# Later factor loads on the second DMA queue, and slot 0's sums in other PSUM banks

## The reference

```python
def _L0_cond_ref(x, w, b):          # depthwise causal conv1d
    y = jax.lax.conv_general_dilated(x, w, window_strides=(1,), padding=[(K - 1, 0)], feature_group_count=D, ...)
    return y + b

def _L0_ffn_ref(x, w_router, w_experts):
    logits = jnp.einsum('bsh,eh->bse', x, w_router)
    idx = jnp.argmax(logits, axis=-1)
    all_out = jnp.einsum('bsh,efh->bsef', x, w_experts)
    return jnp.take_along_axis(all_out, idx[:, :, None, None], axis=2)[:, :, 0, :]

x = x + _L0_ffn_ref(_L0_cond_ref(x, cond_2048[:, None, :], L0_cond_b), L0_ffn_w_router, L0_ffn_w_experts)
```

## Time and profile before

| | |
|---|---|
| median of 3 runs | 513.11 us (511.46, 513.11, 513.98) |
| the profiled execution | 512.61 us |
| its span, first to last instruction | 510.8 us |
| TensorE busy | 502.5 us, 98% |
| VectorE, ScalarE, GpSimd busy | 56%, 29%, 26% |
| convolution, first to last matmul | 4.86 to about 123 us |
| expert slots | 123.51 to about 505 us |
| mean granted TensorE clock | 0.997 |

### The profile page before, as it was taken

One profiled execution on the slowest core, in us unless ns is written; L12 is line 12 of the kernel. 1 busy time (PEld: TensorE's weight loads), 2 busy tenths in 40 slices (PEclk: granted clock), 3 DMA queues, 4 the chain that ended last, 5 costly groups with the idle time before them and its releaser, 6 DMA issues.

```text
span 510.8 us, 9483 instructions
## 1 busy us (share of the span) xinstructions
PE 502.5 (98%) x2764; PEld 435.5 (85%) x2765; DVE 287.6 (56%) x418; ACT 150.5 (29%) x255; POOL 133.2 (26%) x148
## 2 busy tenths in 40 slices
PE   8999999999999999999999999999999999999995
PEld 8999999998888888888888888888888888888884
DVE  4947373769885233599753422863266343472961
ACT  2444444286101001365620000610043010340710
POOL 0004325063622111323311312203122322122222
PEclk9999999999999999999999999999999999999998
DMA  8977999999779999699998664695649655534445
GB/s 290 411 221 212 398 282 405 348 346 309 264 253 283 341 350 299 184 348 358 327 395 249 175 198 123 202 372 177 185 133 354 221 165 158 169 116 130 145 142 165
DMA packets 59623, 130.31 MB, mean 255 GB/s; under 512 B 12752, under 2 KB 32720, under 8 KB 59600
## 3 DMA queue, kind: packets, MB, share of 16 engines
q1 hardware_dynamic: 41696, 70.12, 44.3%
q0 software_dynamic: 14832, 54.27, 29.6%
q10 hardware_dynamic: 3072, 5.65, 3.5%
HBM read 94.56 MB, written 35.45 MB: 255 GB/s over the span
## 4 chain that ended last, share of the span: by engine, by line
PE 93%; DMA 5%; issue 0%; POOL 0%; DVE 0%; DVEq 0%; ACT 0%; SPq 0%; POOLq 0%
PE ps L858 75%; PE ps L814 18%; DMA y_sorted<-rows,pos_i 3%; DMA xs<-x_t 2%; DMA xs<-x_both 1%; POOL out L937 0%; DVEq L167 0%; DVE xs L516 0%; PE ps L829 0%; SPq L307 0%; ACT rows L438 0%; ACT part L437 0%; PE ps L826 0%; POOLq L978 0%; DVE x_row L702 0%
## 5 line engine op out<-in xcount | busy, mean ns | idle before, releaser
L858 PE MATMUL ps<-w_sb,ys 128*128 128x512 f32 x1680 | 381.6, 389 | 0.4 <-ACT rows L438 0.4
L858 PEld LDWEIGHTS ps<-w_sb,ys 128*128 128x128 f32 x1680 | 315.2, 188 | 66.1 <-ACT rows L438 0.5
L689 DVE STREAM_TRANSPOSE y_cols<-y_blk 128x1024 f32<-128x1024 f32 x36 | 44.8, 1243 | 140.1 <-PE ps L858 131.6
L814 PE MATMUL ps<-mats,xs 128*128 128x128 f32 x1024 | 117.8, 278 | 1.4 <-DMA xs<-x_both 1.1
L814 PEld LDWEIGHTS ps<-mats,xs 128*128 128x128 f32 x1024 | 116.9, 195 | 1.9 <-DVE mats L508 1.4
L451 ACT CAST ys<-y_cols 128x1024 fp32r<-128x1024 f32 x36 | 37.9, 1052 | 269.4 <-DVE y_cols L689 269.4
L680 DVE TENSOR_TENSOR w_sb<-w_raw,w_sb 128x1024 fp32r<-128x1024 f32 x56 | 64.2, 1218 | 3.3 <-ACT w_sb L446 3.3
L937 POOL DMA_INDIRECT out<-x_row,idx x35 | 40.8, 1165 | 80.3 <-DVE x_row L704 76.4
L944 POOL COPY idx<-ids_all 128x1 int32 (+1 forms) x36 | 15.2, 421 | 173.5 <-DMA out<-x_row,idx 118.7
L446 ACT CAST w_sb<-w_raw 128x1024 fp32r<-128x1024 f32 x56 | 56.4, 1050 | 9.5 <-PE ps L858 8.6
L925 POOL DMA_INDIRECT y_sorted<-rows,pos_i x32 | 35.3, 1103 | 78.1 <-PE ps L814 74.9
(11 more groups left out here) (102 smaller groups left out, 47.7 us busy)
## 6 DMA issues: line engine op xcount, KB each, us to landing
w_raw<-experts SPq DMA_DIRECT2D x56, 512.0 KB, 9.5
y_blk<-y_sorted SPq DMA_DIRECT2D x152, 128.0 KB, 3.4
xs<-x_both SPq DMA_DIRECT2D x15, 512.0 KB, 9.8
xs<-x_t SPq DMA_DIRECT2D x28, 256.0 KB, 7.0
xs<-x_t ACTq DMA_DIRECT2D x20, 256.0 KB, 7.5
w_first<-experts SPq DMA_DIRECT2D x8, 512.0 KB, 9.7
ids_all<-y_sorted SPq DMA_DIRECT2D x38, 1.0 KB, 4.5
x_row<-x_rows,idx POOLq DMA_INDIRECT x36, 4.6
```

Of the source, the lines that this page charges most:

```text
L689: V.transpose(y_cols[k][:, :, :].rearrange("p m (t i) -> p t m i", t=4), y_blk[k][:, :, :, :]).then_inc(y_blocks, 1)
L814: mm = nc.tensor.matmul(to, xs[:, n % X_RING, s % PACK, :], mats[:, s, :].rearrange("p (u n) -> p u n", n=SIDE), start=(s == sets[0]), sto ...
L858: return nc.tensor.matmul(out_ps[k][:, f * HALF:(f + 1) * HALF], ys[k][:, a, c, :], w_sb[:, c, b, f * HALF:(f + 1) * HALF], start=(c == 0 ...
```

## The change

ACT now waits for the factors of pack 0 to have landed before it asks for those of pack 1 and of packs 2 and 3. The sums of the slots with k = 0, slot 0 first, move from banks 4 and 5 to banks 6 and 7, where the ranks of groups 0 to 2 lie. The ranks of the last group move to bank 4. With this the waits change: slot 0 is entered when the positions of group 2 have been read out of bank 6 (`pos_ready` at 3) and no longer when 72 evictions are done, and the last ranks are begun when all 76 evictions are done, in place of `pos_ready` at 2.

```diff
@@ -229,14 +229,14 @@
-        out_banks = [4, 0]
+        out_banks = [6, 0]
...
         def rank_ps(g):
-            return ps[:, 6 + g % 2, 0:(TPG + 1) * EXPERTS].rearrange("p (t e) -> p t e", t=TPG + 1)
+            return ps[:, 6 + g % 2 if g < LAST else 4, 0:(TPG + 1) * EXPERTS].rearrange("p (t e) -> p t e", t=TPG + 1)
@@ -411,6 +411,7 @@
             act.wait_ge(warm_zero, 2)
             nc.scalar.activation(warm[:, 1:2], warm[:, 0:1], ACT.Identity)
+            act.wait_ge(factors_in[0], 16)
             load_factors(act, 1)
             load_factors(act, 2)
@@ -820,7 +821,9 @@
                 pe.wait_ge(chosen_ready, g + 1)
                 pe.wait_ge(const_in, 16)
-                if g >= 2:
+                if g == LAST:
+                    pe.wait_ge(conv_out, GROUPS * BANKS)
+                elif g >= 2:
 
                     pe.wait_ge(pos_ready, g - 1)
@@ -877,7 +880,7 @@
-            pe.wait_ge(conv_out, GROUPS * BANKS - 4)
+            pe.wait_ge(pos_ready, LAST)
             gemm(0, 0, None)
```

## The result

| | before | after |
|---|---|---|
| median, us (6 runs each, same series) | 513.34 (511.46 to 514.32) | 518.9 (515.55 to 520.87) |
| profiled execution, us | 512.61 | 520.27 |
| its span, us | 510.8 | 518.4 |
| first convolution matmul | 4.86 | 4.03 |
| slot 0 starts | 123.51 | 127.03 |

The kernel became slower: 1.0105 times the time before, interval 1.0065 to 1.0146. That is +5.6 us by the medians, where 0.1 less was forecast; 518.9 lies outside the range. A ratio leaves out the few slow executions and isn't the quotient of the two medians, from which it differs by up to 0.3%.) Of the 7.6 us between the two spans, 3.5 stand before slot 0 and 4.1 behind it (518.4 less 127.03, against 510.8 less 123.51).

The account below looks back on a forecast made before the run. TensorE, busy 98% of the span, was taken as the bound, with 1.5 us of idle time open to change. Profiled 512.61 minus 0.1 (head) minus 0 (slot 0) gave 512.5, or 513.0 us on the median; range 511.2 to 514.8.

Parts of the forecast that it names:

- The first matmul: Head: fewer factor bytes beside x's first half; 0.4 to 0.87 us to gain, 0.6 taken, start 4.26 not 4.86.
- The length of the factors' transfer: Head, ACT's queue: pack 1's factors take 4.4 us beside SP's backlog, landing at 7.2, matrices at 8.6.
- The far bound: Head: pack 1's factors take 5.8 us, as the constants did, landing at 8.6, matrices at 10.0.
- rival 1: Head: factors come in time, the head start lives, perhaps with an earlier clock rise; −0.3 to −1.0 us; chance 0.17.
- The pace: Head: TensorE at 1.2 GHz up to about 9.2; a changed rise counted as nothing in the sum, both signs in range.
- rival 3: Head: late factors, and the pause puts off the clock's rise; +3.2 us, 516.3; chance 0.06.
- part 1: Head: ACT's delayed request for the factors of packs 1 to 3; 0.6 us head start, 0.1 us left after a wait.
- The rule weighed: Head: DMA engines serve queues in turn, packet by packet, so SP's backlog would hardly delay ACT's transfer.
- the near bound: Head: pack 1's factors keep their 3.0 us, landing at 5.8, matrices at 7.2.
- Part 2: Entry into slot 0: the bank moves gain 0, since DVE's token subtraction, not the eviction, ends the 0.36 us wait.
- Rival 4: Entry into slot 0: it did wait for the eviction; 0.36 us less, 512.7; chance only within the forecast's 0.68.
- A head start lives on: Convolution after the head: later loads and scatters move with TensorE, so the 0.1 us carries through unchanged.

Follow-up runs that it names:

- e1: Kernel before plus only ACT's wait for pack 0's factors before asking for those of packs 1 to 3; banks unchanged: 517.78 against 514.13 us, 1.0061.
- e3: The changed kernel with both edits, run once more on the same chip as the others: 518.34 us, 1.0082.
- e15: Kernel before plus only ACT's wait for pack 0's factors, same kernel as e1, one more execution: 517.51 us.
- e10: Kernel before plus ACT's wait for pack 0's factors, and 65 matmuls on zeros between packs 0 and 1: 518.35 us, 1.0088.
- e13: Kernel before plus ACT's wait for pack 0's factors, and 48 matmuls on zeros between packs 0 and 1: 515.97 against 514.4 us, 1.0046.
- e6: Kernel before plus ACT's wait for pack 0's factors, and 30 matmuls on zeros between packs 0 and 1: 518.93 us, 1.0066.
- e5: Kernel before plus ACT's wait for pack 0's factors; SP asks for x pack 1 and later only after pack 1's factors land: 516.86 us, 1.0046.
- e8: Kernel before, but only the factors of packs 2 and 3 wait for pack 0's; pack 1's are asked for at once: 515.37 us, 1.0024.
- e4: Kernel before, but SP asks for the factors of packs 1 to 3, behind the halves of x pack 0, and ACT for none: 515.97 us, 1.0038.
- e2: Kernel before plus only the slot sums' and last ranks' bank moves with their waits: 513.84 against 514.13 us, 1.0000.
- e7: Kernel before, with the first convolution matmul also waiting for x pack 2, a late start: 517.71 against 514.09 us, 1.0072.
- e14: Kernel before with 34 start matmuls on zeros instead of 24: 515.02 against 514.4 us, 1.0023.
- e12: The kernel before, unchanged, profiled again in one execution: 515.61 us.
- e9: As e4, and ACT asks for the constants only after x pack 2 lands, not pack 0: 516.89 against 513.89 us, 1.0034.

## Why the prediction was wrong

- **The first matmul** (forecast 4.26, measured 4.03; 4.01, 3.99 and 4.01 in e1, e3 and e15): right in kind. x's half took 2.7 us, as if all 192 KB were gone from beside it: by the even share that the prediction worked out for that case, 0.87 us were to be had, and 0.83 came. The middle of 0.6 was too careful. In e10, with the same edit, nothing came (3.5 us, first matmul at 4.86), so the even share is not shown as a rule.
- **The length of the factors' transfer** is the step that failed. Taken: 4.4 us, between 3.0 and 5.8. Measured: 6.39, 6.28, 5.92 and 5.96 (after, e1, e3, e15), and 6.6 to 7.1 in e13, e10 and e6. The far bound was the constants' row, and the argument for staying below it was that less was queued on SP at 2.8 than at 6.22. Neither held: the smaller transfer with less queued ahead took longer than the constants had. e5 shows that it is the backlog all the same, 2.0 us without it. The constants' 5.8 us was one sample of that delay, not its upper end (5.9 to 6.4 in other executions of the kernel before), nor was it, as the prediction says, ACT's only other transfer beside a backlog: the marks, behind the constants, took 15.7. The delay is a wait ahead of the first packets, 3.8 us of the 6.4, which the prediction had no term for. Landing 9.10 in place of 7.2, matrices of pack 1 usable at about 10.4 in place of 8.6.
- **Pack 0's end** was put at 8.1 with TensorE at half pace. It was 6.2 in the profile of after, 7.4 in e1, as the clock came up at once or some 3 us into the work, in place of 4.4 us. The earlier rise was foreseen as a gain (rival 1). Here it only lengthened the pause: 4.32 us in after, where 0.5 was forecast.
- **The cover of packs 2 and 3** was given as 0.3 us at worst. The transfer landed at 10.89, not 9.1; it cost nothing beyond the first only because TensorE itself came late. In e8, where pack 1 was in time, it cost 0.27 us.
- **The pace**, put at nothing in the sum, cost 1.6 us (2.6 in e15). In kind this is rival 3, whose condition (a landing later than about 7.9) was met in every profile of part 1. Its price was +3.2 against a measured +3.65 (e1, by its ratio +3.1) and +4.2 (e3); in the first series it was +5.6, and its profile has waits behind slot 0. The make-up was other than worked out, 1.8 of pause and 1.6 of clock for 1.0 and 2.2. So was the way: the rival has the first rise of the clock put off, while in after, e1 and e15 the clock had risen in pack 0 and fell again. That the price came near is in part luck. Its chance of 0.06 rested on the far bound being rare, so the mis-sized transfer is behind this error as well. The Trainium skill, TensorE: Matmul & The Clock Gate, section HAM oscillation, tells of waits on DMA inside the work after which TensorE goes on at half rate. This trace agrees: 0.50 granted and 333 ns loads after 4.32 us of standing still, and the same in e1, e3, e5, e6 and e15. Where the pause was 1.56 us with zero matmuls ahead of it (e13) or 2.40 us (e4) the clock stayed up.
- **The rule weighed** did not keep the transfer near 3.0 us. The Trainium skill, DMA: Bandwidth & Descriptors, section Queues, rings and completion order, has each DMA engine serve the queues in turn, packet by packet. From 6.5 to 9.1 this trace agrees, with 191 packets of ACT's queue beside 197 of SP's. But from 2.7 to 6.5 there were 6 beside 398. The step from the rule to the near bound left out any delay ahead of the first packet. What holds ACT's packets back until then no run here takes apart.
- **Part 2** was right in each step: not the eviction but DVE's subtraction ends the wait, 0.1 us ahead of the first product, the idle time stays, and e2 measures 1.0000 (0.9978 to 1.0023). Rival 4 is refuted with it.
- **"A head start lives on" and shifts pass to the end** held for a delay (e7). For a gain they did not: in e4 (pack 1 of x asked for later), e8 (pack 1 of x late) and e14 (matrices at 17.85) each head start ended at the next late transfer. The cover of what comes later was taken from one execution, in which those transfers were in time for the old start.
- **Behind 128 us** the prediction carried everything through unchanged. The first comparison shows 4.1 us there, of which e12 shows up to 3.4 in the kernel before itself. That is the width of this measurement, and the range allowed only 1.7 below and 0.9 above for it. What starts these waits (the gathers of up to 9.3 us between SP's loads of weights) stays open.

No kernel tried here beats the one before: e2 is at 1.0000, e4, e5, e8, e9, e13 and e14 lie between 1.0023 and 1.0046, and the rest are slower still.

## What to carry to other kernels

A transfer that is asked for later is not the same transfer later: ask what its issuer's neighbours have queued by then, and if the only row for that state comes from a longer queue or a larger transfer, don't take it as an upper bound. A small load that gates the next stage belongs ahead of a backlog of megabytes, even if it slows the first tile by 0.8 us. And price a pause of TensorE near the head with the pace after it: here 1.8 us of waiting brought 1.6 us of half clock.

## What the runs showed of the hardware beside that

- 64 KB on ACT's queue: 3.0 us beside x's first halves, 2.0 with SP silent behind pack 0, 5.9 to 7.1 over seven executions with SP's next packs queued, and in after 3.8 us of it passed with 6 packets moved. The queue's being another one gave it no protection.
- x pack 1, 512 KB, landed at 7.97 before, and at 8.50 (after), 8.72 (e4), 8.93 (e8) and 9.75 (e9). In e4 it was asked for 0.94 us later and took as long as before. In after and e8 it was asked for at the same time as before, and what made it later stays open; so does the further 1.0 us of e9, where it isn't the constants.
- The rise of the clock after the head varies from one execution to the next, with the same start matmuls: weight loads of 192 ns from the first convolution matmul on (after), only from 6.8 (e1), 9.2 or about 16 (e9). Part of what looks like a 1 to 2 us effect of an edit at the head can be that.
